# Unused rows of the keys: one 32-row transfer per half from a block in DRAM

## The reference

```
x = x + 0.5 * ffn(layernorm(x))     # 8 experts, each takes its 128 best tokens of a batch
x = x + attn(layernorm(x))          # 16 heads of width 8
x = x + 0.5 * ffn(layernorm(x))

# attn, for each batch and head
inner, outer, v = (x @ Wi), (x @ Wo), (x @ Wv)
attn = softmax(inner @ outer.T / sqrt(8)) * aperture[q] * expression[k]
attn = attn / (attn.sum(-1) + 1e-8)
converged = attn @ v                # then rotated per head, and @ Wout
```

## Time and profile before

| what | value |
|---|---|
| median of 3 runs | 522.78 us (521.08 to 523.35) |
| profiled execution, its own time | 521.46 us |
| its span | 519.7 us |
| PE busy | 413.0 us (79%) |
| DVE busy | 388.7 us (75%) |
| ACT busy | 236.6 us (46%) |
| POOL busy | 54.3 us (10%) |
| TensorE's granted clock, mean over the span | 0.91 |

### The profile page before, as it was taken

The page is one execution under the profiler, slowest core; times in us unless marked ns, Lnnn a source line. Parts: engine busy times, 40 slices in busy tenths (PEclk is TensorE's granted clock), DMA queues, the critical chain, the costliest instruction groups (busy, mean ns, idle before and its releaser), DMA issues.

```text
span 519.7 us, 7791 instructions
## 1 busy us (share of the span) xinstructions
PE 413.0 (79%) x2252; PEld 221.5 (43%) x2252; DVE 388.7 (75%) x841; ACT 236.6 (46%) x439; POOL 54.3 (10%) x103
## 2 busy tenths in 40 slices
PE   2605999997912899999999999999996506999995
PEld 2501557774501344333333333333443402557773
DVE  6698859897803887888888888888655598768884
ACT  2400443333301116777777777777775201543332
POOL 5510001120000001000000000000002510011100
PEclk9999999999675657999999999999999655999999
DMA  6000001210405480111111111110010000011212
GB/s 164 1 0 1 1 30 62 61 34 28 178 26 194 139 325 27 43 53 45 42 41 41 41 41 41 41 41 1 7 58 0 0 0 2 1 33 58 62 30 81
DMA packets 24935, 26.96 MB, mean 52 GB/s; under 512 B 3778, under 2 KB 16594, under 8 KB 24850
## 3 DMA queue, kind: packets, MB, share of 16 engines
q1 hardware_dynamic: 24912, 26.67, 16.2%
HBM read 17.05 MB, written 9.45 MB: 51 GB/s over the span
## 4 chain that ended last, share of the span: by engine, by line
PE 58%; DVE 21%; issue 11%; DMA 6%; ACT 2%; POOL 1%; SPq 0%; DVEq 0%; POOLq 0%; ACTq 0%
PE ps L1160 12%; PE ps L1134 11%; DVE neg_max L808 8%; PE ps L1150 5%; PE ps L1036 5%; DMA parts_dram<-part_lo 5%; DVE probs L746 4%; PE ps L1019 3%; PE ps L1051 3%; PE ps L1021 2%; PE ps L1020 2%; PE ps L1052 2%; PE ps L961 2%; PE ps L1169 2%; PE ps L1142 2%
## 5 line engine op out<-in xcount | busy, mean ns | idle before, releaser
L808 DVE TENSOR_REDUCE neg_max<-ps 128x1 f32<-128x512 f32 x256 | 163.4, 685 | 36.5 <-PE ps L1134 34.8
L597 ACT ACTIVATE probs<-ps 128x512 f32<-128x512 f32 x256 | 137.1, 592 | 57.4 <-PE ps L1150 56.2
L1134 PE MATMUL ps<-stacks 63*128 63x512 f32 x256 | 88.7, 522 | 27.1 <-DMA stacks<-parts_dram 20.3
L1134 PEld LDWEIGHTS ps<-stacks 63*128 63x128 f32 x256 | 35.5, 197 | 104.1 <-DVE neg_max L808 74.8
L1150 PE MATMUL ps<-stacks 64*128 64x512 f32 x256 | 70.5, 419 | 0.5 <-ACT probs L597 0.5
L1160 PE MATMUL ps<-probs,v_ext 128*32 128x512 f32 x512 | 69.0, 612 | 0.0
L523 ACT CAST stacks<-ps 128x512 fp32r<-128x512 f32 x32 | 17.2, 589 | 67.5 <-PE ps L1000 67.5
L1150 PEld LDWEIGHTS ps<-stacks 64*128 64x128 f32 x256 | 34.1, 191 | 13.4 <-ACT probs L597 10.4
L769 DVE TENSOR_TENSOR vae_and_gates<-heads_out,ps 128x512 f32<-128x512 f32 x32 | 21.9, 687 | 20.6 <-ACT heads_out L531 18.4
L746 DVE TENSOR_TENSOR probs<-slot_row,slot 128x1024 f16<-128x1024 f16 x32 | 36.5, 1221 | 0.1
L451 POOL TENSOR_TENSOR w_lo<-w_gu,w_hi 128x512 fp32r<-128x512 f32 x16 | 20.5, 1288 | 149.7 <-ACT w_hi L510 149.7
(11 more groups left out here) (150 smaller groups left out, 560.2 us busy)
## 6 DMA issues: line engine op xcount, KB each, us to landing
stacks<-parts_dram SPq DMA_DIRECT2D x64, 128.0 KB, 2.4
parts_dram<-part_hi SPq DMA_DIRECT2D x8, 512.0 KB, 4.6
parts_dram<-part_lo SPq DMA_DIRECT2D x8, 512.0 KB, 5.5
w_gu<-in_L_ffn_Wg_dram SPq DMA_DIRECT2D x16, 128.0 KB, 2.1
w_gu<-in_L_ffn_Wu_dram SPq DMA_DIRECT2D x16, 128.0 KB, 2.2
wd_sb<-in_L_ffn_Wd_dram SPq DMA_DIRECT2D x16, 128.0 KB, 2.3
x<-in_L_attn_x_dram SPq DMA_DIRECT2D x4, 256.0 KB, 3.8
out_dram<-x SPq DMA_DIRECT2D x4, 256.0 KB, 2.9
```

Of the source, the lines that this page charges most:

```text
L597: nc.scalar.activation(probs[:, u // HG, u % HG, :], ps[:, RING + ring_bank(step, u), :], ACT.Exp, scale=SCORE_SCALE).then_inc(probs_ready, 1)
L808: nc.vector.tensor_reduce(neg_max[:, g, qt, col:col + 1], ps[:, ring_bank(step, u), :], AX.X, ALU.max, negate=True).then_inc(max_taken, 1)
L1134: nc.tensor.matmul(ps[:, ring_bank(step, u), :], q_stack[rows, g, pp, chunk(qt)], k_stack[rows, g, pp, :], start=True, stop=True).then_inc ...
```

## The change

The tensor in DRAM that held one row of zeros becomes a block of 32 rows of 16 KB. It is written by two transfers early in the program, behind the loads of the attention's parameters: zeros to all of it, then, once these have landed, ones to its last row. The fill then has one transfer per half, 32 rows at once, in place of one for the row of ones and one for the 31 rows of zeros. TensorE's wait counts two transfers instead of four.

```diff
-        zero_row_dram = nc.dram_tensor("zero_row_dram", [1, G * PAIRS * S], F32, kind="Internal").ap()
+        k_rows_dram = nc.dram_tensor("k_rows_dram", [TILE - ROWS, G * PAIRS * S], F32, kind="Internal").ap()
...
+            sp.wait_ge(consts_made, 7)
+            quarter_rows = k_rows_dram.rearrange("r (q n t) -> (r q) n t", q=4, t=S // 2)
+            sp.dma_start(quarter_rows, zeros[:].bitcast(F32).unsqueeze(1).broadcast_to([P, 4, S // 2])).then_inc(k_rows_stored, 16)
+            sp.wait_ge(k_rows_stored, 16)
+            sp.wait_ge(ones_row_made, 1)
+            sp.dma_start(k_rows_dram[TILE - ROWS - 1:TILE - ROWS].rearrange("r (a t) -> r a t", t=64),
+                         ones_row[:].unsqueeze(1).broadcast_to([1, G * PAIRS * S // 64, 64])).then_inc(k_rows_stored, 16)
+
             def load_experts(l):
...
-            sp.wait_ge(consts_made, 7)
-            zero_floats = zeros[0:2 * G * PAIRS].bitcast(F32)
-            sp.dma_start(zero_row_dram.rearrange("a (p t) -> (a p) t", t=S // 2), zero_floats).then_inc(zero_row_stored, 16)
-            sp.wait_ge(zero_row_stored, 16)
-            sp.wait_ge(ones_row_made, 1)
+            sp.wait_ge(k_rows_stored, 32)
             sp.wait_ge(gate_up_done[0], 2 * MI * E)
             for jj in range(2):
-                at = TILE * jj + MAX_ROW
-                sp.dma_start(k_stack[at:at + 1].bitcast(F32).rearrange("r g pp (a t) -> r (g pp a) t", t=64),
-                             ones_row[:].unsqueeze(1).broadcast_to([1, G * PAIRS * S // 64, 64])).then_inc(k_rows_filled, 16)
-                sp.dma_start(k_stack[TILE * jj + ROWS:at].bitcast(F32).rearrange("r g pp t -> r (g pp t)"),
-                             zero_row_dram.broadcast_to([MAX_ROW - ROWS, G * PAIRS * S])).then_inc(k_rows_filled, 16)
+                sp.dma_start(k_stack[TILE * jj + ROWS:TILE * jj + TILE].bitcast(F32).rearrange("r g pp t -> r (g pp t)"),
+                             k_rows_dram).then_inc(k_rows_filled, 16)
             store_parts(0)
...
-            pe.wait_ge(k_rows_filled, 64)
+            pe.wait_ge(k_rows_filled, 32)
```

More of the change, by code:

```diff
@@ L186, in macaron_block @@
         attention_consts = sem("attention_consts")
-        ones_row_made, zero_row_stored, k_rows_filled = sem("ones_row_made"), sem("zero_row_stored"), sem("k_rows_filled")
+        ones_row_made, k_rows_stored, k_rows_filled = sem("ones_row_made"), sem("k_rows_stored"), sem("k_rows_filled")
         x_loaded = [sem(f"x_loaded{b}") for b in range(B)]
```

## The result

The changed kernel takes 498.83 us as the median of four runs (498.48 to 505.28) against 522.15 for the kernel before (521.08 to 523.35): a ratio of 0.958, 95% interval 0.951 to 0.965. Forecast were 500.1, in 496.5 to 503.8. Measured twice more, the same kernel came to 498.61 and 498.58, with ratios of 0.954 (0.950 to 0.959) and 0.957 (0.955 to 0.958).

The account below looks back on a forecast made before the run. A hole in which the core waits for one DMA engine's backlog was taken to bound the kernel. 521.46 less 22.65 us (20.3 stall, 2.3 clock) gives 498.8, put at the median's level as 500.1, range 496.5 to 503.8.

Parts of the forecast that it names:

- The cause of the hole: Between 145 and 157 us the core stands still, because one DMA engine carries both 31-row transfers of the fill.
- Rival C: At the fill, 32 rows also go through one engine, adding 1.3 us of backlog: 524.1 us, chance 0.03.
- The stall: TensorE's wait for the stacks goes: L1134 starts at 144.85 instead of 165.19, 20.3 us earlier.
- Rival B: At L1134 a stall of 3.9 us remains because stores land late: 504.0 us, chance 0.12.
- The clock's 2.3 us: Without the hole project_qk(3) runs at full clock, so the fourth neg_max gains 2.3 us beyond the stall's 20.3.
- Behind it: After the fourth neg_max the clock falls and returns about 10 us into the attention, as before: 0 us.
- rival A: The clock stays at 2.4 GHz through the maxima into the attention: 2.0 us more gained, 498.0 us, chance 0.13.
- rival D: TensorE stays at 1.2 GHz deep into the attention; a clearly slower result needs 25 us lost; chance 0.01.
- The fill's price: The two 32-row transfers take between 2.9 and 19.8 us; the low end was taken, ending by about 121.
- The block, its place and SP's issues: Writing the block early on idle SP, and two fewer DMA issues there, were each priced at 0.
- The level: The sum of 498.8, from the profiled execution, was raised by 1.3 us to the median's level: 500.1.

Follow-up runs that it names:

- experiment 1: The kernel before, with each half's 31 rows of zeros filled by two transfers, of 16 and 15 rows: 499.30 us, ratio 0.958.
- experiment 2: The changed kernel with each half's one fill transfer cut into 31 rows and 1 row: 522.15 us, ratio 0.9998.
- second profile: Profile of the changed kernel, unaltered and run again: an execution of 499.0 us, span 497.3; that run's median was 498.61 us.
- first profile: Profile of the changed kernel from its first measurement: the execution of 505.28 us, span 503.5.
- Experiment 5: The changed kernel with its block prepared at about 107 us, behind the experts' loads, instead of early: 498.96 us, ratio 0.954.

## Why the prediction was right

**The cause of the hole: right, and shown.** It was the backlog of the two transfers of 31 rows, 992 KB. Experiments 1 and 2 turn the gain on and off by the number of rows in a transfer alone; that one of sixteen engines carried it is inferred from the shares, the rates and the sums of bytes. Rival C, that 32 rows go the same way, is out: the share between 122 and 132 us is 0.00.

**The stall: right.** Forecast were stores landed at 140.4 and L1134 at 144.85. The loads behind the stores are issued at 141.04 and 140.25 in the two profiles, L1135 starts at 145.25 and 144.48. Rival B, a rest of the wait, did not come: the longest landing of those stores is 5.5 us, and L1135 had nothing to wait for.

**The clock's 2.3 us: right.** At 145 to 150 us the clock is 1.00, the gap is 0.19 us, and the fourth neg_max stands at 148.36 and 147.59 against 147.85 forecast, so 22.1 and 22.9 us earlier than before, forecast 22.65.

**Behind it: right for most executions.** From the fourth neg_max to the end of the span are 349.2 us in before (519.7 - 170.50), 349.7 in the second profile, but 355.1 in the first. The prediction had set 2 us of change there as a sign of being wrong, and in the first profile the change is 5.9. The clock fell at about 150 us again without a hole, against rival A, and no gap before it was a wait for DMA. In the first profile it came back 18 us later than in the second, which is rival D in a small dose: I had given it a bound of what would be needed, and not thought of 6 us. An execution like that lies outside my range; the median does not. That the clock comes back where it did before was taken over from one trace, with no reason for the time. It held in 14 of 15 runs by their times, and in that part the forecast had luck.

**The fill's price: mis-sized, without effect.** I took 2.9 us for 1 MB at 360 GB/s. It took until about 121, at 152 GB/s on the mean of 115 to 122 us, or some 5.5 us, under the experts' last matmuls as foreseen. By its row of landings the second of the two transfers counts as landed 6.7 us after its issue, so at about 123, still 10 us ahead of the first store. The other end, 19.8 us, was far too high.

**The block, its place and SP's issues: 0, right.** Experiment 5 shows it for the place, experiment 1 for the block.

**The level.** The sum against the profiled execution was 498.8, and I added 1.3 to stand with the median of before. The changed kernel's medians are 498.6 to 498.8, so the sum without the addition was right to 0.2 us, and the addition was the whole error of 1.3 us.

## What to carry to other kernels

When a transfer takes far longer to land than its like elsewhere, look at the DMA share of the quiet stretches around it: 0.06 is the share of one engine of sixteen, and here its backlog held up the four stores that were issued behind it. Count the rows of a large transfer: here 31 in one were far worse than 32, or than 16 and 15, and the bill came later at a store that looks innocent. What such a backlog costs is what sticks out beyond its cover, so halving it did not halve the cost, it took about four fifths of it away (18.1 of 23.5 us by the medians, 18.2 of 22.4 by the spans).

## What the runs showed of the hardware

- At a share of 0.06 to 0.07 the DMA moved 25 to 28 GB/s, in the kernel before and in experiment 2. At shares near 1 the rate depends on what is moved: 364 and 383 GB/s from 138 to 140 us, where only stores ran (before and after), 360 from 145 to 150 in the profile after, 120 in the fill of experiment 1.
